# Band queries and keys projected once with a lane permutation on VectorE, PSUM banks given out singly, mask products on quarters of the array

## The chip, the cores and the metric

The program runs on one core of a Trainium2 chip. A core has five engines that run their own instruction queues in order and meet only at semaphores: TensorE (PE, matrix products into PSUM), VectorE (DVE), ScalarE (ACT), GpSimd (POOL, no access to PSUM) and SyncE (SP, transfers). PSUM has eight banks of 512 fp32 columns on 128 partitions; this kernel uses six of them for short-lived fills and two for the attention context. The metric is the device time of one execution in microseconds.

## The reference

The input x holds 16 sequences of 256 tokens with 128 features. Eight residual steps follow one another, each on the layer norm of x:

```
x = x + band_attention(norm(x))       # 16 heads of 64, bias, rotary (half-split), window of 128 keys back
x = x + ffn0(norm(x))                 # silu(gate) * up, hidden 384
x = x + causal_attention(norm(x))     # 16 heads of 8, rotary
x = x + ffn0(norm(x))
x = x + chunk_attention(norm(x))      # 16 heads of 8, rotary, chunks of 64 tokens
x = x + ffn1(norm(x))                 # hidden 352, operands quantised to FP4 in blocks of 16
x = x + lowrank_attention(norm(x))    # 16 heads, rank 32
x = x + ffn1(norm(x))
```

The rotary embedding of the band attention is `x * cos + concat(-x2, x1) * sin` over the 64 features of a head, where x1 and x2 are its lower and upper 32 features. Scores outside the window are -1e30 before the softmax.

## The kernel before

Work is cut into units: one unit is one kind of attention ("band", "causal", "chunk", "lowrank", and "end" for the last FFN) for one sequence, so 5 x 16 units. A unit has steps in stages: "forward" and "finish" (the FFN that lies ahead of its attention), "operands" (norm, queries, keys, values), "maxima" (a first pass of scores, whose negated row maxima are taken), "back" (scores again, transposed, with the mask and the maxima added in PSUM; exponentials; products with the values) and "tail" (denominators, scaling, output projection). The FFNs ahead of causal and chunk units are ffn0, those ahead of lowrank and end units are ffn1.

Nothing is ordered by hand. `make_plan` simulates the five engines once at build time with the durations of `work` and the waits of `needs`: at each step it takes, of the stages whose next step is ready, the one with the smallest start + PER_UNIT x unit - LEAD[engine][stage][kind]. What comes out is one fixed list of steps per engine (`ORDER`), and for every fill of PSUM its slot. A slot is a pair of banks (1024 columns), there are three (SLOTS), and a fill takes a whole slot even where it writes 256 columns. A fill on PE waits until the step in `released_by` of the slot's last user is done.

Band operands: for each of 8 chunks (two heads each) a step `qk` writes four products of 128 x 256 on PE: queries, queries with the halves of each head swapped (a second copy of the weights, rows permuted on the host), keys, keys swapped. Each product is three matmuls (high and low part of fp32), so 12 for a chunk. DVE (L1242) adds the bias and multiplies by the cosine or sine table in four instructions of 256 columns, POOL (L986) adds the two parts into `band_r`, ACT (L1007) casts them into `band_rb` for the first pass of scores. `band_r` has two buffers, `band_rb` one, so the cast of the next unit waits for this unit's last score fill. DVE runs two chunks ahead of POOL at most (`band_sum`).

Scores: a fill of the first pass ("score", six for a band unit) begins with two mask products (`mm_mask`, one for each bank, 128 x 128 by 512 or 256 columns), then comes a product for each head on 64 rows of the array, even heads on the upper and odd heads on the lower 64, each into a bank of its own. DVE takes the maxima (L1201). The last fill is followed on POOL by `parts` (L937 to L940, the maxima split in three bf16 parts), on PE by `nm` (a transpose). The fills of the second pass ("S", for each group g of four heads one wide and one narrow) have the same mask products, then keys x queries in fp32 and the maxima, and ACT takes the exponential (L1087). "V" is the product with the values and the row sums (`one_col`).

## Time and profile before

| | us |
|---|---|
| median of 3 runs (2148.47 to 2153.92) | 2152.45 |
| the profiled execution | 2152.07 |
| its span, first to last instruction | 2150.2 |
| PE busy | 1789.7 |
| DVE busy | 1345.8 |
| POOL busy | 978.6 |
| ACT busy | 808.8 |

The profile comes from one execution. "Busy" is the time in which an engine had an instruction in work; PEld is the weight load of PE, which overlaps its products. PEclk is the granted TensorE clock as a share of 2.4 GHz; the engine has two levels, 1.2 and 2.4 GHz, so 0.90 means a fifth of the time at 1.2. Products are pipelined, and the durations of single ones overlap: the time from start to start tells what one costs.

### The profile page before, as it was taken

The numbers are of one execution on the slowest core, as the hardware profiler recorded it, in microseconds if no ns is written. First come the engines' busy times: TensorE is split into PE (matmuls) and PEld (weight loads), VectorE is DVE, ScalarE is ACT, GpSimd is POOL, SyncE is SP. The second block draws the span as 40 slices with busy tenths as digits, with TensorE's granted clock in tenths as the row PEclk, the third lists the DMA queues.
The fourth block names the chain that finished last, engine by engine and source line by source line (L and its number), as shares of the span: only waits on it lengthen the run. The fifth ranks groups of instructions, "written<-read, shape, count | busy, mean of one in ns | idle before, by whom it ended". The sixth has DMA issues, their size and how long they took to land.

```text
span 2150.2 us, 51747 instructions
## 1 busy us (share of the span) xinstructions
PE 1789.7 (83%) x21261; PEld 1250.9 (58%) x21261; DVE 1345.8 (63%) x2753; ACT 808.8 (38%) x1303; POOL 978.6 (46%) x1362
## 2 busy tenths in 40 slices
PE   4899889999999998879999997777776778888883
PEld 4566565666666666655555555667665455555553
DVE  4555555555555543574555555677876788888873
ACT  2333333333333332324444444333333444444441
POOL 3333222333332222453333435689997455555543
PEclk9999999999999999989999999888998788888886
DMA  4000000000000000023333332233443223323310
GB/s 161 1 1 1 1 2 1 1 1 1 1 1 1 1 1 1 16 56 74 64 78 71 75 75 61 60 74 78 91 87 65 46 62 65 65 65 65 65 21 8
DMA packets 167465, 89.54 MB, mean 42 GB/s; under 512 B 9393, under 2 KB 165810, under 8 KB 166978
## 3 DMA queue, kind: packets, MB, share of 16 engines
q1 hardware_dynamic: 167010, 85.70, 18.4%
q8 instruction: 172, 2.82, 0.6%
q14 instruction: 59, 0.48, 0.1%
q0 software_dynamic: 224, 0.54, 0.1%
HBM read 46.36 MB, written 39.85 MB: 40 GB/s over the span
## 4 chain that ended last, share of the span: by engine, by line
PE 51%; DVE 27%; ACT 7%; POOL 7%; issue 6%; DVEq 0%; POOLq 0%; ACTq 0%
PE slots L1327 38%; DVE nmx L1201 12%; PE ctx_ps L1327 10%; DVE rope_part L1242 4%; ACT probs L1087 3%; DVE rope_part L1166 2%; PE slots L1615 2%; ACT ctxT L1007 1%; DVE ctxT L1303 1%; DVE rope_part L1167 1%; POOL xn L922 1%; PE slots L1394 1%; ACT band_va L1023 1%; POOL band_rb L645 1%; DVE band_r L1167 1%
## 5 line engine op out<-in xcount | busy, mean ns | idle before, releaser
L1087 ACT ACTIVATE probs<-slots 128x1024 f32<-128x1024 f32 (+1 forms) x416 | 356.1, 892 | 322.0 <-PE slots L1327 318.8
L1201 DVE TENSOR_REDUCE nmx<-slots 128x8 f32<-128x1024 f32 (+2 forms) x352 | 407.7, 1216 | 102.8 <-PE slots L1327 101.2
L1327 PE MATMUL slots<-band_r 64*64 64x64 bf16 (+4 forms) x5120 | 393.6, 263 | 80.5 <-DVE nmx L1201 41.7
L1327 PEld LDWEIGHTS slots<-band_r 64*128 64x128 bf16 (+2 forms) x5120 | 194.6, 120 | 254.3 <-issue 129.8
L1242 DVE SCALAR_TENSOR_TENSOR rope_part<-slots,bias_qk,rope_band 128x256 f32<-128x256 f32 x512 | 212.3, 477 | 197.3 <-PE slots L1327 176.4
L1327 PE MATMUL ctx_ps<-probs,band_va 64*32 64x64 f32 (+4 forms) x5120 | 260.5, 313 | 42.3 <-issue 19.4
L986 POOL TENSOR_TENSOR band_r<-rope_part 128x512 f32<-128x512 f32 x128 | 164.5, 1285 | 250.9 <-DVE rope_part L1242 250.9
L1327 PE MATMUL slots<-mask,ident_bf 128*128 128x256 bf16 (+1 forms) x896 | 217.2, 324 | 46.9 <-DVE nmx L1201 17.7
L1327 PE MATMUL slots<-nmT,pick 64*128 64x256 bf16 (+2 forms) x2560 | 218.7, 241 | 2.7 <-issue 2.7
L1327 PEld LDWEIGHTS ctx_ps<-probs,band_va 128*32 128x32 f32 (+2 forms) x5120 | 145.3, 118 | 125.6 <-issue 62.8
L900 POOL TENSOR_TENSOR var_eps<-mean_var,eps 128x2 f32<-128x2 f32 x128 | 29.2, 228 | 393.4 <-DVE mean_var L1129 393.4
L1327 PE MATMUL slots<-xT,band_qk 128*128 128x256 f32 x1536 | 200.0, 288 | 8.2 <-DVEq L1248 6.1
L1327 PEld LDWEIGHTS slots<-xT,band_qk 128*128 128x128 f32 x1536 | 188.0, 191 | 19.7 <-DVEq L1248 13.6
L1007 ACT ACTIVATE ctxT<-ctx_ps 128x512 f32<-128x512 f32 (+1 forms) x112 | 87.4, 781 | 169.2 <-PE ctx_ps L1327 169.2
L922 POOL TENSOR_SCALAR band_va<-x,mean_var,rstd 128x128 f32<-128x128 f32 x128 | 100.8, 794 | 86.0 <-PE slots L1368 65.9
L1007 ACT ACTIVATE band_rb<-band_r 128x512 bf16<-128x512 f32 x128 | 79.4, 630 | 157.0 <-POOL band_r L986 157.0
L1327 PEld LDWEIGHTS slots<-mask,ident_bf 128*128 128x128 bf16 x896 | 54.9, 97 | 133.8 <-issue 44.9
L1166 DVE SCALAR_TENSOR_TENSOR rope_part<-band_va,slots 128x352 f32<-128x352 f32 (+2 forms) x128 | 68.6, 536 | 81.9 <-ACT band_va L1023 55.5
L1327 PEld LDWEIGHTS slots<-nmT,pick 64*128 64x128 bf16 (+1 forms) x2560 | 102.9, 104 | 11.5 <-issue 2.9
L922 POOL TENSOR_SCALAR xn<-x,mean_var,rstd 128x128 f32<-128x128 f32 x128 | 103.6, 816 | 2.9 <-POOL rstd L901 2.8
L937 POOL CAST nm<-nmx 128x64 bf16<-128x64 f32 x64 | 15.1, 236 | 179.0 <-PE slots L1573 92.7
L901 POOL TENSOR_TENSOR rstd<-var_eps,minus_half 128x2 f32<-128x2 f32 x128 | 91.5, 715 | 10.0
(181 smaller groups left out, 2947.5 us busy)
## 6 DMA issues: line engine op xcount, KB each, us to landing
band_r<-scratch SPq DMA_DIRECT2D x192, 192.0 KB, 4.5
scratch<-parts SPq DMA_DIRECT2D x96, 192.0 KB, 2.2
scratch<-parts SPq DMA_DIRECT2D x96, 128.0 KB, 2.1
scratch<-parts SPq DMA_DIRECT2D x96, 64.0 KB, 1.8
x<-in_x SPq DMA_DIRECT2D x16, 128.0 KB, 4.5
out<-x SPq DMA_DIRECT2D x16, 128.0 KB, 1.8
band_r<-in_band_qk_a SPq DMA_DIRECT2D x1, 1024.0 KB, 6.4
band_va<-in_band_qk_b SPq DMA_DIRECT2D x1, 1024.0 KB, 10.3
```

Source lines behind the costliest of these rows:

```text
L900: link(nc.gpsimd.tensor_tensor(var_eps[:, b], mean_var[:, b, :, 1], eps[:], ALU.add))
L901: nc.gpsimd.tensor_tensor(rstd[:, b], var_eps[:, b], minus_half[:], ALU.pow).then_inc(rstd_ready, 1)
L922: nc.gpsimd.tensor_scalar(xn[:, t, :], x[:, b, t, :], mean_var[:, b, t, 0:1], rstd[:, b, t:t + 1], ALU.subtract, ALU.mult).then_inc(xn_rea ...
L986: nc.gpsimd.tensor_tensor(band_r[:, b % RING, j], part[:, 0], part[:, 1], ALU.add).then_inc(band_sum, 1)
L1007: return nc.scalar.activation(dst, src, ACT.Copy)
L1087: nc.scalar.activation(probs[:, g % 2, step[2], :, 0:width], slot(u, step).rearrange("p (a n) -> p a n", a=2)[:, :, 0:width], ACT.Exp, sca ...
L1166: link(nc.vector.scalar_tensor_tensor(g_out, t_in, 1.0, gate, ALU.add, ALU.mult))
L1167: nc.vector.tensor_tensor(h_out, g_out, up, ALU.mult).then_inc(free_sem(u, ("ffn", i)), 1)
L1201: nc.vector.tensor_reduce(dst, src, axis=AX.X, op=ALU.max, negate=True).then_inc(free_sem(u, step), 1)
L1242: nc.vector.scalar_tensor_tensor(rope_part[:, c % 2, rot, qk, :], slot(u, step)[:, o:o + TOK], bias_qk[:, j, 2 * qk + rot:2 * qk + rot + 1 ...
L1327: return nc.tensor.matmul(o, lhsT, rhs, start=start, stop=stop, skip_group_check=shared)
L1615: last = nc.tensor.transpose(B[:, g * P:(g + 1) * P], ctxT[:, g, t * P:(t + 1) * P], ident[:])
```

## The change

1. **Band queries and keys are projected once.** `qk` now writes two products of 128 x 256 (6 matmuls) into one bank. ACT adds the bias and writes `biased` (two activations of 256 columns, new), POOL multiplies by the cosine (step `cos`, new, 128 x 512), DVE swaps the halves with a lane permutation and multiplies by the sine (step `sin`: STREAM_SHUFFLE and TENSOR_TENSOR, both 128 x 512, instead of four SCALAR_TENSOR_TENSOR of 256), POOL adds as before (now part of `sin`). The permutation reaches 32 lanes, so the host permutes the features of a head, with which the halves lie 16 lanes apart; queries and keys have the same order, and scores don't change by it. `biased` has two buffers, `turned` has one.
2. **Weights**: the staged and split band weights are half as many (2 x 512 KB instead of 2 x 1024 KB).
3. **PSUM is given out in single banks.** A fill for which `narrow` is true takes one of six banks, any other takes a pair. A fill may wait for two earlier ones. There is a semaphore for each pair and each bank.
4. **Mask products on quarters.** Instead of one product of 128 x 128 for each bank there are two of 64 x 64; the four of a fill lie on the four quarters of the array.
5. **The plan's numbers**: the table LEAD, PER_UNIT and the durations for the changed steps are new, and with them the order on every engine.

```diff
-                steps.append(("qk", j))
+                steps += [("qk", j), ("cos", j), ("sin", j)]
...
-        "qk": [("pe", 1.43), ("dve", 1.56), ("pool", 1.21)] if big else [("pe", 0.72 if low else 1.43)],
+        "cos": [("pool", 1.21)],
+        "sin": [("dve", 1.3), ("pool", 1.21)],
+        "qk": [("pe", 0.72), ("act", 0.74)] if big else [("pe", 0.72 if low else 1.43)],
...
-        "operands": {"band": 4.447, "causal": 7.702, "chunk": 18.901, "lowrank": 57.299},
+        "operands": {"band": 0.0, "causal": 0.38, "chunk": -0.093, "lowrank": 3.926},
...
+def narrow(kind, step):
+    name = step[0]
+    if name == "v":
+        return kind != "band"
+    if name == "qk":
+        return kind in ("band", "lowrank")
+    if name == "ffn":
+        return step[1] == 2 and AHEAD[kind] == "ffn0"
+    return name in ("xT", "down", "nm", "den", "rden", "ctx", "ctxT", "out")
...
+                    if step[0] == "cos":
+                        j = step[1]
+                        c = b * CHUNKS + j
+                        if c >= 2:
+                            pool.wait_ge(band_sum, c - 1)
+                        pool.wait_ge(biased_ready, c + 1)
+                        released(pool, u, ("qk", j))
+                        nc.gpsimd.tensor_tensor(rope_part[:, c % 2, 0], biased[:, c % 2], rope["band"][:, 0:1, :].to_broadcast([P, 2, TOK]),
+                                                ALU.mult).then_inc(cosine_ready, 1)
...
+                    if kind == "band" and name == "qk":
+                        j = step[1]
+                        c = b * CHUNKS + j
+                        if c >= 2:
+                            act.wait_ge(band_sum, c - 1)
+                        act.wait_ge(front_full, FRONT_NO[u, step] + 1)
+                        for qk in range(2):
+                            nc.scalar.activation(biased[:, c % 2, qk], slot(u, step)[:, TOK * qk:TOK * (qk + 1)], ACT.Identity,
+                                                 bias=bias_qk[:, j, qk:qk + 1]).then_inc(free_sem(u, step) if qk else biased_ready, 1)
...
-                        for rot in range(2):
-                            for qk in range(2):
-                                o = 512 * qk + TOK * rot
-                                nc.vector.scalar_tensor_tensor(
-                                    rope_part[:, c % 2, rot, qk, :], slot(u, step)[:, o:o + TOK],
-                                    bias_qk[:, j, 2 * qk + rot:2 * qk + rot + 1], rope["band"][:, rot, :],
-                                    ALU.add, ALU.mult).then_inc(part_ready, 1)
...
+                        nc.vector.stream_shuffle(turned[:].rearrange("p q n -> p (q n)"),
+                                                 biased[:, c % 2].rearrange("p q n -> p (q n)"), HALVES_SWAPPED).then_inc(turn_ready, 1)
+                        dve.wait_ge(turn_ready, c + 1)
+                        nc.vector.tensor_tensor(rope_part[:, c % 2, 1], turned[:], twice(rope["band"][:, 1, :]), ALU.mult).then_inc(sine_ready, 1)
...
-                    o = bank.rearrange("p (h w) -> p h w", w=width)[:, :, columns]
-                    rhs = mask[:, allowed].unsqueeze(1).to_broadcast([P, heads, allowed.stop - allowed.start])
-                    mm(o, ident_bf[:], rhs, True, False, shared=True)
+                    for half in range(2):
+                        rows, at = (slice(HALF * i, HALF * i + HALF) for i in (half ^ par, half))
+                        o = bank[at].rearrange("p (h w) -> p h w", w=width)[:, :, columns]
+                        rhs = mask[rows, par, allowed].unsqueeze(1).to_broadcast([HALF, heads, allowed.stop - allowed.start])
+                        mm(o, ident_bf[rows, rows], rhs, True, False, shared=True)
```

How the order moves. First PE in the middle of the band stage; `xT,band_qk` is a unit's projection, `band_r` and `nmT` the second pass of scores, `band_rb` the first. Before, from the last narrow fill of the second pass on (96 matmuls are all eight chunks):

```order
L1327 MATMUL slots<-mask,ident_bf 128x256 x2
L1327 MATMUL slots<-band_r 128x128 x2
L1327 MATMUL slots<-nmT,pick 128x128 x2
L1327 MATMUL slots<-band_r 128x128 x2
L1327 MATMUL slots<-nmT,pick 128x128 x2
L1327 MATMUL slots<-xT,band_qk 128x256 x96
L1327 MATMUL ctx_ps<-probs,band_va 64x256 x2
```

After, from the next unit's transposed norm on (six matmuls are one chunk):

```order
L1426 MATMUL slots<-ident,xn 128x128 x2
L1385 MATMUL slots<-xT,band_qk 128x256 x6
L1630 MATMUL slots<-ident_bf,nm 128x128 x2
L1385 MATMUL slots<-xT,band_qk 128x256 x18
L1385 MATMUL slots<-mask,ident_bf 64x512 x4
L1385 MATMUL slots<-band_r 128x256 x2
L1385 MATMUL slots<-nmT,pick 128x256 x2
L1385 MATMUL slots<-band_r 128x256 x2
L1385 MATMUL slots<-nmT,pick 128x256 x2
L1385 MATMUL slots<-xT,band_qk 128x256 x18
```

The projection has moved from behind the second pass to its head, and lies between its fills.

POOL in the band stage, from the rstd of one unit on; `rope_part` is the chunk's rotary work. Before:

```order
L901 TENSOR_TENSOR rstd<-var_eps,minus_half 128x2
L986 TENSOR_TENSOR band_r<-rope_part 128x512 x8
L900 TENSOR_TENSOR var_eps<-mean_var,eps 128x2
L901 TENSOR_TENSOR rstd<-var_eps,minus_half 128x2
L922 TENSOR_SCALAR xn<-x,mean_var,rstd 128x128 x2
```

After, a piece of one unit:

```order
L1027 TENSOR_TENSOR rope_part<-biased,rope_band 128x512
L1037 TENSOR_TENSOR band_r<-rope_part 128x512
L1027 TENSOR_TENSOR rope_part<-biased,rope_band 128x512
L1037 TENSOR_TENSOR band_r<-rope_part 128x512
L941 TENSOR_TENSOR var_eps<-mean_var,eps 128x2
L942 TENSOR_TENSOR rstd<-var_eps,minus_half 128x2
```

Each chunk has two POOL instructions of 512 columns where it had one.

PE at the end of the band stage; `int_gu` and `int_d` are ffn0, ahead of the causal units. Before, in the last band unit's second pass:

```order
L1327 MATMUL slots<-int_d,rope_part 128x128 x6
L1327 MATMUL slots<-xTf,int_gu 128x256 x12
L1368 MATMUL slots<-ident,band_va 128x128 x2
L1327 MATMUL slots<-mask,ident_bf 128x256 x2
L1327 MATMUL slots<-band_r 128x128 x2
L1327 MATMUL slots<-nmT,pick 128x128 x2
```

After, behind that second pass:

```order
L1385 MATMUL slots<-int_d,rope_part 128x128 x6
L1385 MATMUL slots<-band_o,ctxT 128x128 x16
L1426 MATMUL slots<-ident,xn 128x128 x2
L1385 MATMUL slots<-xTf,int_gu 128x256 x12
L1385 MATMUL slots<-xT,causal_qkv 128x256 x12
L1385 MATMUL slots<-causal_qkv,xT 128x128 x6
```

Before, fifteen ffn0 stand between the maxima of the last band unit and those of the first causal unit; after, three and a half do, and the rest lie between the causal units. Counted in the order of PE by where the transpose `nm` of each unit stands (ffn0 and ffn1 in each stretch):

| stretch of PE's order | before | after |
|---|---|---|
| last band `nm` to first causal `nm` | 15 ffn0 | 3 ffn0 |
| first causal to first chunk | 9 ffn0 | 15 ffn0 |
| first chunk to first lowrank | 8 ffn0, 15 ffn1 | 13 ffn0, 5 ffn1 |
| first to last lowrank | 15 ffn1 | 25 ffn1 |
| after the last lowrank | 2 ffn1 | 2 ffn1 |

## Rows read from the trace of the kernel before

**Rows 1.** Windows: length, PE, PEld, DVE, ACT, POOL busy, clock, DMA share, GB/s

```profile
551.05:601.58 50.53, 47.33 (x440) 32.37 (x440) 26.15 (x58) 16.76 (x27) 15.35 (x20) 1.00 0.01 1
803.50:947.40 143.90, 117.78 (x1056) 90.47 (x1057) 75.33 (x190) 40.84 (x84) 57.48 (x84) 0.94 0.07 16
947.40:1299.60 352.20, 317.99 (x3778) 191.97 (x3778) 199.50 (x370) 160.44 (x261) 134.53 (x213) 1.00 0.34 72
1299.60:1675.00 375.40, 275.17 (x6435) 239.92 (x6434) 277.23 (x657) 136.58 (x253) 294.75 (x407) 0.88 0.36 74
1675.00:2086.90 411.90, 329.79 (x3295) 213.03 (x3292) 334.17 (x558) 197.30 (x290) 218.32 (x318) 0.86 0.28 58
2086.90:2150.20 63.30, 29.43 (x235) 22.60 (x233) 29.51 (x61) 15.71 (x25) 25.94 (x36) 0.69 0.02 7
```

**Rows 2.** POOL's cast of the maxima: all 64, then the third and last band unit's

```profile
L937 POOL CAST nm<-nmx x64: 230/236/238, 62.1 to 2086.9; 128x64 bf16<-128x64 f32 x64
...
131.96 0.24 POOL L937 CAST nm<-nmx 128x64 bf16<-128x64 f32 x1 [7.11 <-PE slots L1573]
...
803.55 0.24 POOL L937 CAST nm<-nmx 128x64 bf16<-128x64 f32 x1 [10.10 <-PE slots L1573]
```

**Rows 3.** Groups by line and shape: busy us, mean ns, idle before

```profile
L1242 DVE SCALAR_TENSOR_TENSOR rope_part<-slots,bias_qk,rope_band 128x256 f32<-128x256 f32 x512 | 212.3, 477 | 197.3 <-PE slots L1327 176.4 <-DVE rope_part L1242 20.9
L1327 PE MATMUL slots<-xT,band_qk 128*128 128x256 f32 x1536 | 200.0, 288 | 8.2 <-DVEq L1248 6.1 <-DVE xT L1142 2.0
L986 POOL TENSOR_TENSOR band_r<-rope_part 128x512 f32<-128x512 f32 x128 | 164.5, 1285 | 250.9 <-DVE rope_part L1242 250.9
L1201 DVE TENSOR_REDUCE nmx<-slots 128x4 f32<-128x1024 f32 x256 | 296.7, 1215 | 22.3 <-PE slots L1327 20.9 <-DVE rope_part L1258 0.2 <-DVE band_va L643 0.2
L1007 ACT ACTIVATE xT<-slots 128x256 fp32r<-128x256 f32 x64 | 24.6, 384 | 39.3 <-PE slots L1368 38.8
L1303 DVE TENSOR_TENSOR ctxT<-slots,ctxT 128x512 f32<-128x512 f32 x64 | 40.0, 682 | 36.0 <-PE slots L1327 36.0
L1327 PE MATMUL slots<-xTf,int_gu 128*128 128x256 f32 x384 | 59.9, 305 | 2.9 <-DVE nmx L1201 1.8 <-DVE xTf L1142 0.2
L1327 PE MATMUL slots<-int_d,rope_part 128*128 128x128 f32 x384 | 53.8, 294 | 4.5 <-DVE rope_part L1167 3.8 <-DVE x L1317 0.3 <-DVE ctxT L1303 0.2
```

**Rows 4.** Timeline of PE in a band unit's second pass: start us, us

```profile
614.63 0.86 PE L1327 MATMUL ctx_ps<-probs,one_col 128*32 128x256 f32 x16
615.42 0.60 PE L1327 MATMUL slots<-mask,ident_bf 128*128 128x512 bf16 x2
615.96 0.70 PE L1327 MATMUL slots<-band_r 64*128 64x256 f32 x4
...
617.25 0.39 PE L1327 MATMUL slots<-mask,ident_bf 128*128 128x256 bf16 x2
617.57 0.49 PE L1327 MATMUL slots<-band_r 64*128 64x128 f32 x4
```

**Rows 5.** Timeline of DVE in a band unit's projection: two chunks

```profile
627.24 1.66 DVE L1242 SCALAR_TENSOR_TENSOR rope_part<-slots,bias_qk,rope_band 128x256 f32<-128x256 f32 x4 [0.21 <-DVE rope_part L1242]
...
629.11 1.66 DVE L1242 SCALAR_TENSOR_TENSOR rope_part<-slots,bias_qk,rope_band 128x256 f32<-128x256 f32 x4 [0.21 <-DVE rope_part L1242]
```

**Rows 6.** By line, ns min/median/max; then DVE and POOL at one moment

```profile
L939 POOL CAST nm<-nmx_d x64: 236/236/956, 62.7 to 2087.5; 128x64 bf16<-128x64 f32 x64
L639 DVE TENSOR_TENSOR band_va<-band_va x32: 424/679/949, 1370.5 to 2114.3; 128x256 f32<-128x256 f32 x32
...
1452.05 0.89 DVE L639 TENSOR_TENSOR band_rb<-band_r,band_rb 128x704 f32<-128x704 f32 x1
1452.08 0.95 POOL L939 CAST nm<-nmx_d 128x64 bf16<-128x64 f32 x1
```

**Rows 7.** Lowrank stretch by tile, DVE fourth number: band_rb, then band_va

```profile
1675.00:2086.90 411.90, 6.02 (x28) 2.91 (x28) 52.03 (x90) 0.00 (x0) 89.05 (x104) 0.86 0.28 58
...
1675.00:2086.90 411.90, 72.30 (x960) 27.96 (x960) 69.33 (x112) 18.26 (x42) 51.17 (x70) 0.86 0.28 58
```

180 lines of the change are left out of this document (105 added, 75 removed).

## The prediction

> **What bounds the kernel now.** I read the busy time by window first, with windows cut at POOL's casts of the row maxima (L937), of which each attention unit has one. The first comes at 62.1 us, the third at 131.96, the sixteenth, of the last band unit, at 803.55, the last at 2086.9 [rows 2]. In the middle of the band stage a unit takes 50.53 us, and PE is busy 47.33 of them at full clock, DVE 26.15, ACT 16.76, POOL 15.35 [rows 1]: PE is the bound there, at 0.937 of the time. The causal stretch is the same (318.0 of 352.2 us, 0.903, clock 1.00). The chunk stretch isn't: POOL has 294.8 and DVE 277.2 of 375.4 us; nor is the lowrank stretch, where DVE has 334.2 and PE 329.8 of 411.9 us, at a granted clock of 0.86 [rows 1]. So PE work that goes counts in the first 1300 us; behind that the order counts.
>
> **Projection.** Half of 1536 matmuls go. Each costs 200.0/1536 = 0.130 us of PE [rows 3], 48 go for a unit: 6.25 us. On DVE a chunk had four instructions in 1.66 us, and came every 1.87 us [rows 5]. Now a chunk has two ACT activations of 256 columns at 0.384 (an activation of that size from PSUM, [rows 3]), so 0.77 us, 6.1 for a unit; ACT then has 23 of some 44 us, and its cost is covered. On POOL a second instruction of 1.285 us joins the first [rows 3]: 10.3 us more for a unit, POOL then 25.6 us. On DVE the product with the sine has 512 columns, 0.68 us by the nearest row, L1303 [rows 3]. The trace has no STREAM_SHUFFLE. Its lower bound is half of that row, 0.34, its upper bound POOL's 1.285 for as many columns; it reads one operand of the same width on DVE, so I take 0.65, nearest to the DVE row. That is 1.33 us for a chunk; at the bounds DVE would have 1.02 or 1.97, and for a unit 24 to 31 us, still not the bound.
>
> **The new chain.** POOL's two instructions and DVE's product are on one chain, and I don't think that they overlap. At 1452.05 a DVE product with two SBUF operands starts; POOL's cast of 0.24 us that starts 0.03 behind it takes 0.95, until the other has ended; and the same DVE product of 256 columns takes between 0.424 and 0.949 us [rows 6]. Before, the rotary products of DVE had one operand in PSUM and POOL's sums kept to 1.285. Now each chunk has a DVE product with two SBUF operands, and POOL reads SBUF all the time. So a chunk takes 2 x 1.285 + 0.68 = 3.25 us, not 2.57, and eight take 26.0 us, not 20.6.
>
> The Trainium skill, page SBUF — State Buffer, section Who interferes with whom, states just this: a DVE instruction with two SBUF inputs and a GpSimd instruction that reads SBUF exclude one another for the whole instruction. The trace agrees, with the 0.95 us above. A rule that lets them run beside each other gives the first rival's time below.
>
> What stands in that chain: the first chunk's matmuls and activations (0.78 + 0.77, so 1.5 us), eight chunks (26.0), and, as `band_rb` is single and PE's order has most of a unit's projection behind the last unit's scores, the rest of DVE's work, 26.15 - 8 x 1.66 = 12.9 us (six maxima at 1.215 and the scaling). Sum 40.4; the maxima's split on POOL, the casts and the exponentials that stand behind casts in ACT's queue add some 3.5. I take a band period of 44 us. PE alone gives less: 47.33 - 6.25 - 2.7 (masks, below) = 38.4, over 0.937 is 41.0 us. So in the band stage the bound moves from PE to the POOL/DVE chain, and PE idles an eighth of the time.
>
> **Masks.** The two products of a wide fill take 0.54 us to the start of what follows (615.42 to 615.96), of a narrow one 0.32 (617.25 to 617.57) [rows 4]. Quarters on different rows and columns can run at once if they behave as the row sums do, 16 records of `one_col` on four column strips in 0.79 us [rows 4]. Then a wide fill needs one pass: half of 0.54, and something for two more loads: 0.32, saved 0.22. Narrow: saved 0.12. Bounds: nothing saved (two pairs one behind the other), or 0.1 us more for each fill for the extra loads, and at best half, 0.27. A band unit has 10 wide and 4 narrow fills: 2.7 us; a causal unit 2 and 12: 1.9 us.
>
> A rule against it: the Trainium skill, page TensorEngine Tiling (Array Packing), section Key Properties, says that a change of tiling mode drains the array. The rows have such a change already, from 128 x 128 masks to products on 64 rows, inside the 0.54 us, so I count no further one.
>
> **Setup.** The split of the band weights is halved. It was in the first 62 us; DVE and ACT work on 2 x 1024 columns less. I take 4 us off, bounds 0 and 8.
>
> **Order and banks.** The table of stretches in the change shows where FFNs go. One ffn0 costs PE (59.9 + 53.8)/32 = 3.55 us [rows 3], with its transposes 4. One ffn1 costs DVE some 10: 52.0 + 69.3 us on two tiles for 15 of them is 8.1 [rows 7], the rest I estimate. Its PE cost lies between an ffn0's 4 and these 10; I take 6.5. Single banks (`narrow`) take away waits for slots; of these PE has few before (idle 8.2 us before the projection, [rows 3]), so I give them nothing beyond the shares below.
>
> **The sum**, stretch by stretch:
> - to the last band cast: 62.1 - 4 + 70 (the first two periods fill the pipeline and stay: 131.96 - 62.1) + 13 x 44 = 700 (before 803.5)
> - last band to first causal cast: PE had 117.8 us with 15 ffn0. Without 12 of them (48), a tail that now lies earlier (5) and masks (2.7) 62 are left; at 0.9 that is 70 (143.9)
> - causal: (318.0 - 9 x 4)/16 - 1.9 = 15.7 a unit; 16 x 15.7 + 15 x 4 = 311; over 0.903: 345 (352.2)
> - chunk: PE 275.2 - 10 x 6.5 + 5 x 4 = 230, above DVE's and POOL's, which lose ten ffn1; at 0.88: 262 (375.4)
> - lowrank: DVE 334.2 + 10 x 10 = 434. At the share of before, 0.81, it takes 535; DVE and PE are loaded more evenly, so 0.83: 523 (411.9)
> - end: 63 (63.3)
>
> Together 1963 us of span. The profiled execution took 2152.07, 1.9 more than its span and within 0.4 of the median of the runs, 2152.45; so I forecast **1965 us**, 187 less than before.
>
> **Rivals.**
> 1. *The products don't exclude each other.* A chunk then takes 2.57 us and PE bounds the band: 13 x (44 - 41) = 39 us less; with a lowrank stretch as tight as the causal one (434/0.88 = 493) 30 less again: 1896. For it: the order interleaves chunks and fills, so a late chunk may hide. Against it: rows 6. 0.20.
> 2. *The quarters give nothing.* This is the case where a part doesn't do what it says. Causal + 1.9 x 16/0.9 = 34 us; the band unit's PE goes to 41.1, over 0.937 is 43.9, so little there, 1 us a unit: 2012. 0.12.
> 3. *The plan was made with wrong prices.* It counts 1.3 and 1.21 us for steps that block each other, and ACT, strictly in order, has activations of the projection between exponentials. Band period 48 (+52), lowrank at 0.81 and a lower clock (+20): 2037. 0.15.
> 4. *Slower.* The projection chain doesn't overlap with the second pass at all: in some units of the new order ACT does all eight chunks of a unit in a row. If all units went so, a period would be 26.0 + 12.9 + some 20 for the second pass, about 59; and where PE idles that long its clock falls (0.86 and 0.94 in stretches where PE is busy 0.80 and 0.82 of the time, [rows 1]), which adds 3. At 62 the span is 234 more, so 2199. It is slower from a band period of about 59 on. Against it: PE's order has chunks between the fills in most units. 0.08.
>
> The forecast itself has 0.45, with 1930 to 2010 as its own range.
>
> **Range and chances.** 1890 to 2075 holds the forecast, rivals 1 and 2 and nearly all of 3. A measurement tells 0.3%, 6.5 us, from no change. Faster 0.88, within 0.3% 0.03, slower 0.09 (rival 4, and the tail of 3).
>
> **What would show it.** The last band cast near 700 us, band periods of 44, PE busy some 38.5 in one; POOL's or DVE's instruction in pairs of which one lasts longer than alone (DVE's product above 0.68, POOL's above 1.285) shows the exclusion, both at their lengths refutes it. Mask groups: from their start to what follows 0.32 instead of 0.54. Causal periods near 21.5 us, chunk 16, lowrank near 35. The forecast is wrong if the first pass waits long for the last cast in every unit, or if the lowrank stretch passes 550 us.

## The result, and the profile after

The changed kernel takes 2207.52 us (median of 4 runs, 2198.63 to 2212.92) against 2152.42 of the kernel before beside it: ratio 1.0249, 95% interval 1.0221 to 1.0278. It is slower by 2.5%, where 1965 us had been forecast. The profiled execution took 2198.63 us, the shortest of the four, with a span of 2196.8.

By stretch, cut at the same casts of the row maxima (before, forecast, after):

| stretch | before | forecast | after |
|---|---|---|---|
| start to last band cast | 803.5 | 700 | 844.0 |
| to the first causal cast | 143.9 | 70 | 65.8 |
| to the first chunk cast | 352.2 | 345 | 359.7 |
| to the first lowrank cast | 375.4 | 262 | 304.3 |
| to the last lowrank cast | 411.9 | 523 | 541.9 |
| to the end | 63.3 | 63 | 81.1 |

The bands are 144 us over the forecast, all that follows 90 us over it, and 6 us over before.

Windows of the changed kernel (columns as in [rows 1]): three neighbouring band units, then the stretches of the table.

```profile
477.80:535.50 57.70, 50.03 (x515) 35.43 (x510) 35.89 (x66) 25.00 (x49) 29.21 (x30) 0.97 0.01 1
535.50:606.10 70.60, 51.97 (x483) 34.35 (x481) 47.04 (x77) 33.89 (x64) 52.90 (x48) 0.86 0.00 1
606.10:628.70 22.60, 22.31 (x274) 13.36 (x272) 6.11 (x6) 9.25 (x15) 1.07 (x5) 0.98 0.01 1
...
844.00:909.80 65.80, 51.17 (x490) 38.00 (x490) 31.03 (x63) 17.04 (x33) 27.40 (x36) 0.88 0.17 42
909.80:1269.50 359.70, 325.75 (x4401) 211.69 (x4402) 217.34 (x421) 170.42 (x280) 142.09 (x227) 0.97 0.31 69
1269.50:1573.80 304.30, 220.59 (x5936) 192.48 (x5938) 195.05 (x453) 110.55 (x203) 192.47 (x289) 0.88 0.40 88
1573.80:2115.70 541.90, 393.74 (x3688) 257.30 (x3688) 398.84 (x787) 215.16 (x337) 321.91 (x450) 0.82 0.21 46
2115.70:2196.80 81.10, 47.19 (x406) 33.50 (x404) 32.79 (x80) 26.36 (x39) 34.42 (x45) 0.77 0.03 9
```

Band casts no longer come evenly: gaps of 57.7, 70.6 and 22.6 us, 50.3 on average, as long as the 50.53 of [rows 1]. PE is busy (50.03 + 51.97 + 22.31)/3 = 41.4 us of such a unit, 5.9 less than before. It waits 8.9 instead of 3.2. So the matmuls went, and waiting took their place; the granted clock, 1.00 before, is 0.86 in the long gap. The full period of 13 units, from the third cast to the last, is (844.0 - 159.7)/13 = 52.6 us.

Groups by line and shape (busy us, mean ns, idle before), the new operations of a chunk:

```profile
L1027 POOL TENSOR_TENSOR rope_part<-biased,rope_band 128x512 f32<-128x512 f32 x128 | 201.2, 1572 | 105.9 <-ACT biased L1100 105.9
L1305 DVE TENSOR_TENSOR rope_part<-turned,rope_band 128x512 f32<-128x512 f32 x128 | 174.7, 1365 | 4.4
L1037 POOL TENSOR_TENSOR band_r<-rope_part 128x512 f32<-128x512 f32 x128 | 162.8, 1272 | 43.9 <-DVE rope_part L1305 19.2 <-issue 10.8 <-ACT biased L1100 4.1
L1100 ACT ACTIVATE biased<-slots,bias_qk 128x256 f32<-128x256 f32 x256 | 106.8, 470 | 151.9 <-POOL band_r L1037 91.6 <-PE slots L1385 59.6
L1302 DVE STREAM_SHUFFLE turned<-biased 128x512 f32<-128x512 f32 x128 | 94.4, 738 | 0.6
```

The timeline of DVE in one of the bursts (start us, us):

```profile
546.44 1.77 DVE L1305 TENSOR_TENSOR rope_part<-turned,rope_band 128x512 f32<-128x512 f32 x1
548.67 0.01 DVE L1302 LOAD_MASK_SELECT turned<-biased  x1 [0.46 <-ACT biased L1100]
548.69 0.75 DVE L1302 STREAM_SHUFFLE turned<-biased 128x512 f32<-128x512 f32 x1
549.47 1.76 DVE L1305 TENSOR_TENSOR rope_part<-turned,rope_band 128x512 f32<-128x512 f32 x1
```

and that of POOL there:

```profile
547.61 1.73 POOL L1027 TENSOR_TENSOR rope_part<-biased,rope_band 128x512 f32<-128x512 f32 x1
549.42 1.26 POOL L1037 TENSOR_TENSOR band_r<-rope_part 128x512 f32<-128x512 f32 x1
550.64 1.72 POOL L1027 TENSOR_TENSOR rope_part<-biased,rope_band 128x512 f32<-128x512 f32 x1
```

A chunk comes every 3.03 us (547.61 to 550.64), against 1.87 in [rows 5]. DVE's product at 549.47 starts 0.05 us behind POOL's sum, which keeps to 1.26 us; the product takes 1.76 and lies across the start of POOL's next product, which takes 1.72. So it is the one that starts later which lasts longer, each time: DVE's product beside the sum, then POOL's product beside DVE's. The sums (L1037) stay between 1.26 and 1.31 us in the whole kernel.

PE around that burst, and the quarter masks in the next pass:

```profile
538.08 1.66 PE L1385 MATMUL slots<-xT,band_qk 128*128 128x256 f32 x12
542.63 0.64 PE L1385 MATMUL slots<-mask,ident_bf 64*64 64x512 bf16 x4 [2.90 <-ACT biased L1100]
543.21 1.23 PE L1385 MATMUL slots<-band_r 64*128 64x256 f32 x4
...
603.52 0.64 PE L1385 MATMUL slots<-mask,ident_bf 64*64 64x512 bf16 x4 [8.92 <-ACT band_rb L1058]
...
611.77 0.41 PE L1385 MATMUL slots<-mask,ident_bf 64*64 64x512 bf16 x4
612.11 0.70 PE L1385 MATMUL slots<-band_r 64*128 64x256 f32 x4
...
613.39 0.30 PE L1385 MATMUL slots<-mask,ident_bf 64*64 64x256 bf16 x4
613.63 0.49 PE L1385 MATMUL slots<-band_r 64*128 64x128 f32 x4
```

The same four products take 1.23 us behind the wait of 2.90, where the granted clock is 0.50 (the lower of its levels, 1.2 GHz), and 0.70 at 612.11, where it is 1.00. The longest wait is that of 8.92 us at 603.52: the first pass of scores waits for the last cast of a chunk. It comes once in three units (also at 452.17 with 7.59 us and at 756.30 with 8.92), in the long gap. There PE's order has all eight projections of a unit, from 572.89 on, behind one second pass and ahead of the next, so that their chain runs to 603.4 with no second pass beside it. A wide mask group now takes 0.34 us to what follows, a narrow one 0.24, against 0.54 and 0.32 in [rows 4].

### The profile page after: what moved, and what is told of

Same layout as the page of the kernel before. It is cut to its first block, busy times and chain, and to the rows that moved or that the text cites. A ratio compares the mean times of both kernels' runs of the same rounds, so it can differ in the third digit from the quotient of the medians.

```text
span 2196.8 us, 52690 instructions
## 1 busy us (share of the span) xinstructions
PE 1708.4 (78%) x21389; PEld 1186.9 (54%) x21389; DVE 1383.7 (63%) x2625; ACT 900.9 (41%) x1559; POOL 1171.4 (53%) x1490
## 4 chain that ended last, share of the span: by engine, by line
PE 45%; DVE 27%; POOL 9%; issue 8%; ACT 6%; DMA 1%; SPq 1%; DVEq 0%; POOLq 0%; ACTq 0%
PE slots L1385 32%; PE ctx_ps L1385 10%; DVE nmx L1261 10%; POOL band_r L1037 3%; ACT probs L1147 2%; POOL rope_part L1027 2%; DVE rope_part L1305 2%; PE slots L1452 2%; DVE rope_part L1226 1%; DVE turned L1302 1%; DVE stats L1186 1%; PE slots L1426 1%; ACT band_r L1058 1%; DVE band_rb L679 1%; DVE band_rb L676 1%
## 5 line engine op out<-in xcount | busy, mean ns | idle before, releaser
L1385 PE MATMUL slots<-band_r 64*64 64x64 bf16 (+4 forms) x5120 | 412.5, 273 | 104.8 <-DVE nmx L1261 67.0
L1027 POOL TENSOR_TENSOR rope_part<-biased,rope_band 128x512 f32<-128x512 f32 x128 | 201.2, 1572 | 105.9 <-ACT biased L1100 105.9
L1385 PE MATMUL slots<-mask,ident_bf 64*64 64x256 bf16 (+1 forms) x1792 | 166.4, 361 | 91.1 <-ACT band_rb L1058 41.9
L1385 PE MATMUL slots<-nmT,pick 64*128 64x256 bf16 (+2 forms) x2560 | 213.4, 240 | 0.0
L1037 POOL TENSOR_TENSOR band_r<-rope_part 128x512 f32<-128x512 f32 x128 | 162.8, 1272 | 43.9 <-DVE rope_part L1305 19.2
L1305 DVE TENSOR_TENSOR rope_part<-turned,rope_band 128x512 f32<-128x512 f32 x128 | 174.7, 1365 | 4.4
L1100 ACT ACTIVATE biased<-slots,bias_qk 128x256 f32<-128x256 f32 x256 | 106.8, 470 | 151.9 <-POOL band_r L1037 91.6
L1385 PEld LDWEIGHTS slots<-mask,ident_bf 64*64 64x64 bf16 x1792 | 52.3, 105 | 186.8 <-issue 114.9
L1058 ACT ACTIVATE ctxT<-ctx_ps 128x512 f32<-128x512 f32 (+1 forms) x112 | 87.5, 781 | 107.3 <-PE ctx_ps L1385 107.2
L963 POOL TENSOR_SCALAR band_va<-x,mean_var,rstd 128x128 f32<-128x128 f32 x128 | 107.6, 848 | 37.6 <-PE slots L1426 35.5
L1385 PE MATMUL slots<-xT,band_qk 128*128 128x256 f32 x768 | 118.7, 307 | 8.5 <-DVE xT L1202 5.0
L1385 PEld LDWEIGHTS slots<-xT,band_qk 128*128 128x128 f32 x768 | 104.5, 206 | 20.4 <-issue 9.8
```

Of the source, the lines that this page charges most:

```text
L963: nc.gpsimd.tensor_scalar(xn[:, t, :], x[:, b, t, :], mean_var[:, b, t, 0:1], rstd[:, b, t:t + 1], ALU.subtract, ALU.mult).then_inc(xn_rea ...
L1027: nc.gpsimd.tensor_tensor(rope_part[:, c % 2, 0], biased[:, c % 2], rope["band"][:, 0:1, :].to_broadcast([P, 2, TOK]), ALU.mult).then_inc( ...
L1037: nc.gpsimd.tensor_tensor(band_r[:, b % RING, j], part[:, 0], part[:, 1], ALU.add).then_inc(band_sum, 1)
L1058: return nc.scalar.activation(dst, src, ACT.Copy)
L1100: nc.scalar.activation(biased[:, c % 2, qk], slot(u, step)[:, TOK * qk:TOK * (qk + 1)], ACT.Identity, bias=bias_qk[:, j, qk:qk + 1]).then_ ...
L1305: nc.vector.tensor_tensor(rope_part[:, c % 2, 1], turned[:], twice(rope["band"][:, 1, :]), ALU.mult).then_inc(sine_ready, 1)
```

## The experiments

The median of the kernel before moved between 2152 and 2158 us from one set of runs to the next, so the table gives each kernel's ratio to the runs of before beside it. The fourth and fifth columns are of the profiled execution: the last band cast, and the span left behind it.

| kernel | ratio | 95% interval | last band cast | rest |
|---|---|---|---|---|
| before | 1 | | 803.5 | 1346.7 |
| after | 1.0249 | 1.0221 to 1.0278 | 844.0 | 1352.8 |
| b_quarters | 0.9937 | 0.9913 to 0.9962 | 796.0 | 1341.6 |
| b_quarters_banks | 1.0383 | 1.0346 to 1.0420 | 793.7 | 1442.4 |
| a_old_lead | 1.0965 | 1.0920 to 1.1009 | 923.8 | 1433.0 |
| a_no_sine | 1.0092 | 1.0060 to 1.0123 | 804.8 | 1365.0 |
| a_sum_only | 0.9868 | 0.9847 to 0.9890 | 754.7 | 1368.1 |
| a_full_mask | 1.0416 | 1.0377 to 1.0454 | 858.3 | 1381.3 |
| a_interleaved | 1.0538 | 1.0492 to 1.0585 | 838.2 | 1428.8 |
| a_interleaved_filled | 1.0574 | 1.0551 to 1.0596 | 844.3 | 1434.8 |
| a_products_swapped | 1.0459 | 1.0427 to 1.0492 | 870.9 | 1382.9 |
| a_repriced | 1.0276 | 1.0232 to 1.0320 | 863.9 | 1354.0 |
| a_late_old_lead | 1.0435 | 1.0407 to 1.0464 | 841.2 | 1408.7 |
| a_paired_banks | 1.1055 | 1.1030 to 1.1080 | 854.8 | 1526.2 |
| b_qb_same_order | 0.9850 | 0.9825 to 0.9876 | 789.9 | 1333.2 |
| a_same_order | 1.0468 | 1.0445 to 1.0491 | 923.9 | 1332.6 |
| own_band_old_late | 1.0083 | 1.0054 to 1.0111 | 844.0 | 1333.8 |
| own_products | 0.9651 | 0.9623 to 0.9679 | 772.7 | 1311.2 |
| order_old_late | 0.9794 | 0.9771 to 0.9816 | 793.1 | 1320.1 |
| order_old_late_2 | 0.9491 | 0.9467 to 0.9515 | 740.8 | 1307.7 |

### Parts of the change on the kernel before

**b_quarters** takes the masks alone.

```
-                    o = bank.rearrange(...)[:, :, columns]
-                    mm(o, ident_bf[:], rhs, True, False, shared=True)
+                    for half in range(2):
+                        rows, at = (slice(HALF * i, HALF * i + HALF) for i in (half ^ par, half))
+                        mm(bank[at]..., ident_bf[rows, rows], rhs, True, False, shared=True)
```

> The kernel before with one part of the change alone: the mask products on quarters of the array. Order, banks and projections are those of before. Theory A (part is worth what its fills show): in the changed kernel a wide mask fill lasted 0.34 us from its start to the next product's, against 0.54 before, a narrow one 0.23 against 0.32; a band unit has 10 wide and 4 narrow fills, so 2.0 + 0.4 = 2.4 us a unit, 38 us in 16 units, and about half as much a unit in the causal stretch, 15 us: about 2100 us. Rival: the freed time of TensorE falls where it waits for VectorE anyway: 2140 to 2152 us, with the band period still 50.5.

It gave 0.6%, some 13 us. The 2143.6 us lie in the rival's range, but its unchanged period of 50.5 isn't found, and theory A's 2100 isn't reached. The windows of two band units:

```profile
595.40:644.80 49.40, 45.35 (x469) 32.35 (x470) 26.13 (x58) 16.67 (x26) 15.35 (x19) 1.00 0.01 1
644.80:694.20 49.40, 45.33 (x469) 32.35 (x470) 26.14 (x58) 16.67 (x26) 15.35 (x19) 1.00 0.01 1
```

The timeline of PE has the wide fills of the second pass 4.91 us apart; in the kernel before they came 5.20 apart, from 615.42 in [rows 4] to the first line here:

```profile
620.62 0.61 PE L1327 MATMUL slots<-mask,ident_bf 128*128 128x512 bf16 x2
```

```profile
611.94 0.41 PE L1327 MATMUL slots<-mask,ident_bf 64*64 64x512 bf16 x4
...
616.85 0.41 PE L1327 MATMUL slots<-mask,ident_bf 64*64 64x512 bf16 x4
```

The period falls from 50.5 to 49.4: that is the four second-pass pairs, 4 x 0.29 = 1.2. The six wide fills of the first pass give nothing, though PE does them faster, since each is followed by a maximum of 1.215 us on DVE [rows 3]. The causal stretch gives nothing either: PE is busy 309.9 us of it instead of 318.0, and it lasts 352.0 instead of 352.2.

**b_quarters_banks** adds the single banks and the rule by which the plan gives them out (`narrow`, with its semaphores); the band's projection keeps a pair.

> The kernel before with the quarter mask products and with the banks given out singly; band queries and keys still with four projections, LEAD and prices of the plan as before. The plan orders the work anew, since narrow fills take one bank. Theory A (banks alone bring nothing, and only the order that the planner makes of them can move the time): within 1.5% of the kernel with quarters alone, so 2070 to 2130 us. Theory B (the old LEAD was fitted to the old rule for the slots, and a new order under it is worse): over 30 us slower than with quarters alone. Theory C (single banks free TensorE of waits for a slot): over 20 us faster than quarters alone.

**b_qb_same_order** has the same operations and banks, but each engine's steps in the order of the kernel before, held fixed: a step is a candidate only if it is the next in a stored list.

```
+                if (u, step) != FIXED[eng][len(order[eng])][1:]:
+                    continue
```

> The kernel before with quarter masks and single banks, and the order of every engine's steps held fixed as in the kernel before; only which bank a fill takes follows the new rule. Under the same LEAD but with a free order it took 2240, with quarters alone 2144. Theory A (the 96 us were the order that the plan made of the new rule, not the banks): 2125 to 2150, and chunk, lowrank and end together near 850 again. Theory B (the banks themselves cost, for instance since a wide fill needs two neighbours free at once): over 2180.

Theory B of the first stood: 1.038. Theory A of the second: 0.985, another 0.9% below the quarters alone. The banks don't cost, they give a little (causal stretch, first to last cast: 331.4 to 325.0). The 5.4% between the two kernels are the plan's order alone, made from the same numbers under another rule for the slots. **a_paired_banks**, the reverse (`narrow` always false in the changed kernel, with its own LEAD), says it again:

> The changed kernel with every fill taking two banks, as the kernel before did; LEAD, operations and prices as in the changed kernel, the order made anew by the plan. Theory A (single banks let TensorE run ahead, and with pairs it waits for slots): last band cast 20 us or more later than 844, TensorE's waits for ScalarE's biased chunk longer. Theory B (single banks bring the band nothing; with three pairs it has the same order of chunks): last band cast within 15 us of 844. The later stretches come to another order, so the whole (2200 to 2310) says less than the band stretch.

The last band cast agrees with theory B, 854.8 and 844.0; the whole is 8% above the changed kernel, and 173 of its 184 us of span lie behind the bands. The order of the bands isn't that of the changed kernel, though: the casts come evenly here, 51.2 us apart in the middle, without a wait of PE over 2.2 us there, and the period is no shorter. So it isn't the unevenness that costs.

### The changed operations in old orders

**a_old_lead** is the changed kernel with the old LEAD and PER_UNIT.

```
-        "operands": {"band": 0.0, "causal": 0.38, "chunk": -0.093, "lowrank": 3.926},
+        "operands": {"band": 4.447, "causal": 7.702, "chunk": 18.901, "lowrank": 57.299},
 (and so all of LEAD)
-PER_UNIT = 0.0185
+PER_UNIT = 0.01
```

> The changed kernel, with the numbers LEAD and PER_UNIT of the kernel before: all changed operations, another order. Theory A (the new order is what costs): the band casts come evenly again, without pairs of units 70 and 23 us apart, the band period falls to 44 to 46 us and the time to 2060 to 2130. Theory B (the operations cost the time, the order is only their consequence): the chunk pace stays 3.0 us, the band period 50 or more, the time 2200 or more. Both keep VectorE's sine product at about 1.4 us and GpSimd's cosine product at 1.6 us on average.

**a_same_order** holds the old order fixed instead; ScalarE's new step is put where its matmuls end.

> All changed operations in the order of the kernel before, held fixed; the new ScalarE step of a chunk is put where its products of TensorE end in that order. With the old LEAD and a free order it took 2364, with a band period of 58.0. Theory A (the chain of chunks costs 8 us a unit where it lies behind the second pass, as one block; the rest of the time is the order's): band period 57 to 58, last band cast about 920, behind it 1340 to 1360 as in the kernel before, the whole 2260 to 2285. Theory B (ScalarE's and GpSimd's new work disturbs the later stages too): the stretches behind the last band cast over 1400 us together.

Theory B of the first, A of the second: band period 58.0, last band cast 923.8 and 923.9. In the fixed order the rest is 1332.6, the same as without the projection's change (1333.2); so the projection touches nothing behind the bands. This pair, b_qb_same_order and a_same_order, prices the new projection by itself in the old order: 0.9850 to 1.0468, a loss of 135 us between the medians, all of it ahead of the last band cast (789.9 to 923.9). The window of one unit of a_old_lead:

```profile
576.00:634.00 58.00, 44.67 (x420) 28.53 (x421) 31.07 (x51) 22.64 (x42) 27.93 (x27) 0.82 0.00 1
```

and PE's timeline in it, from the block of eight projections on:

```profile
596.69 5.95 PE L1385 MATMUL slots<-xT,band_qk 128*128 128x256 f32 x48
...
612.08 0.28 PE L1630 MATMUL slots<-ident_bf,nm 128*128 128x128 bf16 x2 [1.50 <-ACT biased L1100]
615.04 2.92 PE L1385 MATMUL slots<-band_v,xT 128*128 128x512 f32 x6 [2.68 <-DVE rden L1354]
...
623.21 0.40 PE L1385 MATMUL slots<-rdT,wide_pick 64*128 64x256 bf16 x2 [3.16 <-DVE ctxT L1361]
625.17 0.64 PE L1385 MATMUL slots<-mask,ident_bf 64*64 64x512 bf16 x4 [1.56 <-ACT band_rb L1058]
```

All eight chunks are projected by 602.6, but the first pass, which needs the last cast, starts at 625.2. The chain runs on in between, and the last unit's scaling stands behind its chunks in DVE's queue and ACT's. Before, the same block cost PE 12 us and the chain 8 x 1.87 = 15; now it costs PE 6 and the chain 24. What PE saved it waits for, and more, at half clock.

### What the chain costs in the changed kernel's own order

**a_no_sine** leaves out the sine product, **a_sum_only** the cosine product too.

```
-   stream_shuffle(turned, ...)
-   tensor_tensor(rope_part[:, c % 2, 1], turned[:], twice(rope["band"][:, 1, :]), ALU.mult)
+   stream_shuffle(rope_part[:, c % 2, 1], ...)
```

> The changed kernel in its own order, with the sine product of the bands left out: the shuffle writes its result where the product would have been written. Only VectorE's operation that reads two SBUF tiles beside GpSimd's products is gone. Theory A (VectorE's and GpSimd's products hold each other up): GpSimd's cosine product falls from 1.72 to 1.26 us although nothing of GpSimd's was changed, the pace of the chunks from 3.03 to about 2.55, the stretch to the last band cast by about 60 us (8 x 0.5 us a unit), the time to 2130 to 2150. Theory B (GpSimd's 1.72 us is its own length for an operand that is broadcast): the cosine product stays at 1.72, the pace near 3.0, the time within 15 us of 2207. Theory C (the order makes the stalls, not the products): the pace falls as in A, but the time falls by less than 20 us.

> The changed kernel in its own order, with both products of the bands left out: ScalarE adds the bias, VectorE shuffles, GpSimd adds the two. GpSimd's work on a chunk falls from 3.0 to 1.3 us, VectorE's from 2.5 to 0.75; TensorE's and ScalarE's stay. Prices the whole chain of the chunks, where leaving out the sine product alone gave 30 us. Theory A (the chain of chunks is what TensorE waits for in the band stretch): last band cast at 720 to 750 instead of 844, band period 43 to 45 as forecast, the whole 2090 to 2120. Theory B (TensorE waits mostly for the first pass, VectorE's maxima and the tail, which are untouched): last band cast 780 to 805, little better than the 804.8 without the sine product, the whole 2150 to 2175. Both: the stretches behind the bands change by less than 20 us.

```profile
L1027 POOL TENSOR_TENSOR rope_part<-biased,rope_band 128x512 f32<-128x512 f32 x128 | 163.4, 1276 | 116.9 <-ACT biased L1100 116.9
```

Without DVE's product POOL's, which nothing else was done to, takes 1276 ns on average instead of 1572 (a_no_sine, group by line), although the shuffle still runs beside it. That settles the exclusion. Leaving the sine product out, which takes away its own time too, is worth 39 us of band stretch, 844.0 to 804.8, less than the 60 of theory A; the whole came to 2178, above the 2130 to 2150 of that theory. Both products are worth 89 us, 844.0 to 754.7, and 3.7% of the whole: nearer to theory A, though the last band cast (720 to 750 expected) and the whole of 2126 (2090 to 2120) both lie above its ranges.

**a_full_mask** takes the quarters out of the changed kernel, its order unchanged.

> The changed kernel in its very order, with the mask products over the full array as before. On the kernel before the quarters gave 13 us, of which 1.1 us a band unit (four wide and four narrow second-pass fills, 4 x 0.29), while the six first-pass fills gave nothing since VectorE's maxima set their pace. Theory A (the same here): 2215 to 2225. Theory B (in the changed kernel TensorE waits more, so the quarters give less): within 5 us of 2207. Theory C (busier TensorE holds its clock): faster than 2205.

1.0416 against 1.0249, so they are worth 36 us here, three times what they gave before. No theory had that. The profiled executions put 14 us of it in the bands, 13 in the causal stretch (372.8 against 359.7, where PE is busy 341.6 us instead of 325.8) and 17 in the chunk stretch (321.4 against 304.3). The 17 aren't all the masks': a_no_sine, which behind the bands has the operations and the order of the changed kernel, took 314.3 there, at a clock of 0.83 instead of 0.88.

### Other orders

**a_repriced** asks whether the plan's wrong prices did it (a chunk counted 1.3 us on DVE, where it takes 2.1 to 2.5).

> The changed kernel, with the prices of the band's steps in its plan set to what the trace showed (cosine 1.76, shuffle and sine product 2.53, sum 1.29, ScalarE's bias pair 0.90, projection 0.81, score 0.67, second pass 1.62 and 0.96), and LEAD found anew for these prices. Every instruction is unchanged, only the order differs. Theory A (the order was fitted to prices 1.2 us too low a chunk, and that is what costs): 2130 to 2175. Theory B (no order of this kind gains back what the longer chunk costs): within 1% of 2207.

Theory B: 1.0276, no better than the changed kernel. The plan's own arithmetic had promised 32 us (its simulated end with the new prices is 2039.7 us under the changed kernel's LEAD and 2007.5 under the new one).

**a_late_old_lead** puts the old LEAD under the chunk, lowrank and end steps only.

> The changed kernel with the old LEAD for the kinds chunk, lowrank and end, and its own for band and causal. Tells what the new order does behind the bands. Theory A (the new order moves feed-forward work from the chunk into the lowrank stretch, where TensorE's clock is lower and VectorE fuller, and loses by it): chunk, lowrank and end together, 954 us in the changed kernel and 911 with all numbers old, come to 900 to 925, the whole to 2155 to 2180. Theory B (the sum of the work is the same and only its place changes): within 15 us of 2207.

Neither: the chunk stretch grew from 304.3 to 380.8 us and the end from 81.1 to 107.2, the lowrank stretch shrank from 541.9 to 504.9, and the rest grew to 1408.7. **own_band_old_late** did the same with the order itself, not the numbers that make it.

> The changed kernel's operations and its own order of all band steps, word for word; behind the bands the steps follow one another on each engine as in the kernel before. Theory A (each stretch stands alone): last band cast 840 to 850 as in the changed kernel, the rest 1325 to 1345 as in b_qb_same_order (1333), the whole 2170 to 2195. Theory B (the changed kernel's order behind the bands is as good as the old one, only laid out otherwise): within 10 us of 2207.

Theory A, by all its numbers: 844.0, 1333.8 and a median of 2173.4 us. So LEAD's numbers aren't a description of an order. In these runs they held for one set of prices and rules, and every kernel that took them over to another was slower than the one they came from.

**a_interleaved** lets TensorE project chunk j only behind fill j of the unit before's second pass.

```
+        if kind == "band" and name == "qk" and u:
+            yield u - 1, ("S", step[1] // 2, step[1] % 2), "pe"
```

> The changed kernel with one rule more in its plan, and the band's operand steps given 3 us more lead: TensorE may project chunk j of a band unit only after fill j of the unit before's second pass. So the eight projections are neither one block behind the second pass (as with the old numbers, period 58.0) nor a burst ahead of it (as in the changed kernel, gaps of 70, 23 and 58), but one to each fill. All operations and their lengths stay. Theory A (the chain of chunks, 8 x 3.03 = 24.3 us, costs only where TensorE has no other work beside it): the second pass, about 27 us of TensorE's time, covers it, and the band period falls from 50.4 on average to 46 to 49 us, the last band cast from 844 to 780 to 800. Theory B (the products' exclusion costs the same wherever they lie, since VectorE and GpSimd are needed by the pass too): period 50 to 52. The order of the later stages changes too, so the band stretch is what tells them apart; the whole by A is 2140 to 2190.

**a_interleaved_filled** repeats products of the scaling in it.

```
-                        for cc in range(2):
+                        for cc in (0, 1, 0, 1, 0, 1):
```

> The interleaved kernel, where TensorE does each of the four bands' scale products (the spread of the reciprocals) three times instead of once, with the same result: 16 more 64x256 products a unit, just where TensorE waits for VectorE ahead of the output projection. In the interleaved kernel that projection took 6.50 us behind four waits of 0.2 to 0.95 us, in the kernel before 3.84. Theory A (the granted clock falls to half after these waits, and that costs 2.7 us a unit): the projection takes 3.84 to 4.5 us, the band period falls from 50.2 to 47.5 to 49, the last band cast from 838 to 800 to 825, although work was added. Theory B (the repeated products lie on the path of the scale chain, VectorE waits for each, and the clock falls anyway at the fills before): period 50.5 to 52.

By their numbers both are theory B: period 50.2, last band cast 838.2, and 51.2 and 844.3 with the filling products. A window of a_interleaved, one unit:

```profile
592.00:642.60 50.60, 43.43 (x422) 30.19 (x423) 31.04 (x51) 22.21 (x42) 27.97 (x27) 0.90 0.00 1
```

PE's timeline at its output projection, with that of the kernel before ahead of it:

```profile
608.39 3.84 PE L1327 MATMUL slots<-band_o,ctxT 128*128 128x128 f32 x32
```

```profile
592.65 6.50 PE L1387 MATMUL slots<-band_o,ctxT 128*128 128x128 f32 x32 [0.95 <-DVE ctxT L1363]
```

and the same in a_interleaved_filled:

```profile
590.91 1.42 PE L1387 MATMUL slots<-rdT,wide_pick 64*128 64x256 bf16 x12 [0.46 <-DVE ctxT L1363]
593.21 6.10 PE L1387 MATMUL slots<-band_o,ctxT 128*128 128x128 f32 x32 [0.88 <-DVE ctxT L1363]
```

The second pass was dense now, from 599.74 on 27.5 us without a wait of PE, and the chain lay beside it. But the unit's end was left thin: the reciprocals, the scaling and the output projection with nothing between them, and the projection ran mostly at half clock (0.56 granted on average in these 6.5 us), 6.50 us where it takes 3.84 at full. Ahead of it PE waited five times in some 4 us, for 0.31 to 0.95 us. More products there didn't bring the clock back (6.10, at 0.61), but they didn't fill all: waits of 0.56, 0.46 and 0.88 us were left. So that remedy fell, and what the half clock costs a unit isn't shown by it. order_old_late and what follows it put other work there instead.

**a_products_swapped** removes the exclusion and leaves nothing out: DVE makes the cosine product, from PSUM as the kernel before did, POOL the sine product.

```
-   POOL: rope_part[:, c % 2, 0] = biased * cos
-   DVE:  turned = shuffle(biased); rope_part[:, c % 2, 1] = turned * sin
+   DVE:  rope_part[:, c % 2, 1] = shuffle(biased); rope_part[:, c % 2, 0, qk] = (slot + bias) * cos
+   POOL: rope_part[:, c % 2, 1] *= sin
```

> The changed kernel with the two products exchanged: VectorE makes the cosine product with the bias, straight from PSUM, in two instructions as the kernel before did (477 ns each), and the shuffle, while GpSimd makes the sine product in place and the sum. No VectorE instruction of the chunk then reads two SBUF tiles. The bank is freed by VectorE instead of ScalarE, so the plan differs at a few places. Theory A (exclusion gone): GpSimd's product takes 1.28 us, VectorE's two 0.48 each, the chunk pace is 2.55 us instead of 3.03, the last band cast 30 to 45 us earlier than 844 and the whole 2150 to 2180, as with the sine product left out. Theory B (what is gained on the pair is lost since the bank is held longer, until VectorE has read it): pace 2.55, but TensorE waits more for a bank, and the whole is over 2195.

The whole went up, by theory B's number, but not for its reason as far as I can tell: with another engine freeing the bank the plan made another order (band gaps of 78, 83 and 23 us), and two things had changed at once.

**order_old_late** and **order_old_late_2** combine what had held: products exchanged, chunk j behind fill j - 1, the steps behind the bands in the old order, held fixed.

> Products exchanged (as in a_products_swapped), projections interleaved with the second pass (chunk j one fill later than in a_interleaved), prices of the bands' steps by the trace, and behind the bands the order of the kernel before held fixed. Theory A (the loss behind the bands was the order's, and pace 2.55 with interleaving lets the chain lie beside the second pass): last band cast 740 to 790, behind it 1335 to 1365, the whole 2080 to 2150. Theory B (the band period stays at 50, since TensorE's clock falls in the thin stretch ahead of the output projection, as in a_interleaved): last band cast 830 or later, the whole 2170 to 2200.

> As order_old_late, with LEAD for the bands found by a search on the plan's own arithmetic: TensorE's output projection of a unit lies one fill earlier, and the last band units meet the causal ones earlier. Theory A: 20 to 40 us below order_old_late. Theory B (the plan's arithmetic doesn't know the clock, so what it gains isn't there on the chip): within 15 us of order_old_late.

**own_products** has the order of the second, but the change's own operations.

> The order of every engine as in order_old_late_2, held fixed, with the very operations of the changed kernel (GpSimd the cosine product, VectorE the sine product with two SBUF operands, the bank freed by ScalarE). Theory A (where the chain lies beside the second pass, its pace hardly counts): pace 3.03 us instead of 2.65, band period 44 to 45.5 instead of 43.6 to 45.1, the whole 2055 to 2080. Theory B (the exclusion costs its full price in any order: 8 x 0.4 = 3.2 us a unit): period 47 to 48, the whole 2095 to 2115.

order_old_late came to 2114.9 us, ratio 0.9794, in theory A's range, with its last band cast (793.1) just above the range and the rest (1320.1) below it. order_old_late_2 came to 2050.5, ratio 0.9491, 64 us lower, more than theory A's 20 to 40. own_products came to 2083.8, ratio 0.9651. order_old_late_2 is 5.1% faster than the kernel before and 7.4% faster than the changed one. Two band units of it, by window:

```profile
522.00:609.20 87.20, 81.01 (x834) 54.41 (x833) 47.91 (x108) 43.50 (x80) 50.19 (x53) 0.96 0.01 2
```

POOL's two operations of a chunk, in its timeline:

```profile
544.68 1.27 POOL L1213 TENSOR_TENSOR rope_part<-rope_part,rope_band 128x512 f32<-128x512 f32 x1
546.09 1.29 POOL L1217 TENSOR_TENSOR band_r<-rope_part 128x512 f32<-128x512 f32 x1
547.33 1.27 POOL L1213 TENSOR_TENSOR rope_part<-rope_part,rope_band 128x512 f32<-128x512 f32 x1
```

and PE's timeline at a unit's end:

```profile
566.86 0.60 PE L1566 MATMUL slots<-mask,ident_bf 64*64 64x512 bf16 x4
...
571.49 0.97 PE L1566 MATMUL slots<-xT,band_qk 128*128 128x256 f32 x6
572.78 3.81 PE L1566 MATMUL slots<-band_o,ctxT 128*128 128x128 f32 x32 [0.31 <-DVE ctxT L1542]
```

A unit takes 43.6 us here, PE is busy 40.5 of them, and in a row the chunks come every 2.65. The next unit's first fill (566.86) and one more chunk of projection (571.49) now stand ahead of the output projection, which begins there at 572.78 and runs at full clock, 3.81 us. It is the fill that has the half clock here (0.60 for its masks). With the change's own products, whose pace is 3.03, the last eight periods are 46.6 us on average against 44.1: 2.5 of the 3.0 us that the exclusion adds to eight chunks show, even in an order that mostly hides the chain. That lies between its two theories, by the period and by the whole.

So the 7.4% between the changed kernel and the best one split in three steps: 1.0249 to 1.0083 for the order behind the bands, to 0.9651 for the order of the bands, to 0.9491 for the exchange of the products. The middle step also moves where the last bands meet the causal units (22.6 of its us lie behind the last band cast), and the last one also changes which engine frees the bank, so it isn't the exclusion alone.

## Why the prediction was wrong

**The operations: right.** The pace of a chunk was put at 3.25 us, with the exclusion, and is 3.03. The shuffle was put at 0.65, and takes 0.74. DVE's sine product takes 0.69 when it is alone and up to 1.8 beside POOL, POOL's cosine product 1.26 alone and 1.72 beside DVE. A pair of activations takes 0.84 us, not 0.77. The mask groups came to 0.34 and 0.24, where 0.32 and 0.20 were forecast. Rival 1 (no exclusion) is refuted, and rival 2 (the quarters give nothing) too. One side sum was wrong and changed nothing: at its bounds DVE would have had 12.9 + 8 x 1.02 = 21 to 12.9 + 8 x 1.97 = 29 us a unit, not 24 to 31.

That agrees with the rule of the Trainium skill, page SBUF — State Buffer, section Who interferes with whom, which was cited ahead of the result; the timelines at 546.44 to 549.34 show it on both sides, as longer instructions and not as idle time. The drain at a change of tiling mode (the Trainium skill, page TensorEngine Tiling (Array Packing), section Key Properties) doesn't show as a cost: the group of four quarter products is shorter than that of the two full ones, 0.34 against 0.54. Both groups are followed by products of another mode, so no run here shows the drain by itself.

**The band period: the step that failed.** "What stands in that chain" added 1.5 + 26.0 + 12.9 + 3.5 to 44 us, as if the chain and DVE's other work were one row, and PE's second pass, some 20 us, always lay beside it. That holds only if the order puts it there. The changed kernel's doesn't: in every third unit all eight chunks lie behind one second pass and ahead of the next, PE waits 8.92 us for the last cast at 603.52, the granted clock is 0.82 from 580 to 606, and three units take 151 us. In the old order, where the chain lies so in every unit, the period is 58.0. Leaving both products out of the chain gave 89 us of the stretch back (a_sum_only), and another order of the bands alone, with the operations as they are, 71 (own_band_old_late to own_products, 844.0 to 772.7). Periods of 43.6 to 45 do exist, in order_old_late_2, with the operations of a chunk sped up, and 46.6 with them as they are, late in the stretch (47.8 over all 13 periods). So the forecast's number was near what the operations allow and had nothing in it for the order that they got, although the order stood in the document and rival 4 had read it: "ACT does all eight chunks of a unit in a row". Rival 4 was judged by how many units go so in full and given 0.08. Its time, 2199, is right by accident: it had the bands at a period of 62 and the rest at the forecast, where the trace has 50.3 and 90 us more behind them.

**Two smaller terms of the band stretch.** The first two periods were kept at 70 us and the first cast put at 58; they took 92 and 67.75, so the third cast came at 159.7, 32 us late. And 13 periods were all counted as steady ones, though in the kernel before the mean of the 13 is (803.55 - 131.96)/13 = 51.7 against 50.5: the units that also prepare the weights of the feed-forward take 54 to 57. That is 15 us that the forecast dropped. Together the stretch came 144 us late: 32 at the third cast and 13 x (52.6 - 44) = 112 behind it.

**Masks.** Each fill saves what was forecast, and a unit was given 2.7 us for it. On the kernel before it gave 1.1, as the first pass waits for DVE's maxima; that those six fills have cover was in the rows ([rows 3], 1215 ns each) and not in the sum. A causal unit was given 1.9 us, 30 in the stretch; b_quarters shows 8 us less of PE there and 0.2 less of time, and a_full_mask against the changed kernel 16 and 13.

**Setup.** 4 us were taken off, and the first cast came 5.6 us later than before. Its order had changed too, so the setup's own gain isn't told by that.

**Behind the bands.** Band to causal was right (70 forecast, 65.8). Causal was 15 us too low: its share was right, 325.75/359.7 = 0.906, but PE had 311 us in the sum and 325.75 in the trace, which is what the mask term took off too much. Chunk failed most: 262 forecast, 304.3 measured. PE's 220.6 us there are near the 230 of the sum, but they are 0.72 of the stretch and not 0.88. The 0.88 has no row as a busy share: PE had 275.17/375.4 = 0.73 before, DVE 0.74 and POOL 0.79, and 0.88 stands in [rows 1] only as the granted clock of that stretch. With 0.73 the sum would have given 314 us. So PE's share of before did hold there, and the step that failed is the share that was put in its place, some 50 us of the sum. Lowrank was 19 us too low, by two errors against each other: DVE has 398.8 us and not 434 (the ten ffn1 more cost it 6.5 us each, not 10), and its share is 0.74 and not 0.83, where it was 0.81 before. The end came 18 us over its 63, with 47.2 us of PE in it instead of 29.4. In the lowrank stretch the clock is 0.82. Two lines of the kernel before, then three of the changed one:

```profile
1896.20 0.39 PE L1327 MATMUL slots<-band_r 64*128 64x256 bf16 x4 [0.74 <-DVE nmx L1201]
1897.34 0.39 PE L1327 MATMUL slots<-band_r 64*128 64x256 bf16 x4 [0.74 <-DVE nmx L1201]
```

```profile
1829.95 1.03 PE L1385 MATMUL slots<-band_r 64*128 64x256 bf16 x8 [3.57 <-DVE nmx L1261]
1832.19 0.61 PE L1385 MATMUL slots<-band_r 64*128 64x256 bf16 x4 [1.21 <-DVE nmx L1261]
1833.33 0.61 PE L1385 MATMUL slots<-band_r 64*128 64x256 bf16 x4 [0.52 <-DVE nmx L1261]
```

Score fills stand there in a row, each behind a maximum of DVE, and take 0.61 us at half clock for what took 0.39. That costs nothing at this place: the fills start 1.14 us apart in both kernels, since DVE's maxima set their pace. What does cost in this stretch isn't shown. What the new order behind the bands costs in all is measured: with the old one there the ratio falls from 1.0249 to 1.0083, 34 us between the medians, and the rest in the profiled executions from 1352.8 to 1333.8. The other 70 us between 1334 and the forecast's 1263 no kernel here found; the lowest rest is 1307.7.

**Rival 3**, wrong prices in the plan, was the nearest in spirit (0.15, 2037). Prices by the trace and new numbers to go with them changed nothing, 1.0276. What the plan's arithmetic lacks isn't told by its prices alone; the half clock behind waits is one thing that it has no term for.

**What stays open.** Why the quarters save time in the changed kernel's causal stretch and not in that of the kernel before, why DVE's share fell in the lowrank stretch, why the added products didn't restore the clock in a_interleaved_filled, and how much of the 90 us of the band order is clock and how much waiting.

## What to carry to other kernels

An operation that leaves the bound engine is worth what the order lets it be: ask which chain its replacement makes, how long that chain is for one unit, and which work of the bound engine is placed beside it, and read this from the new order row by row before taking the sum of busy times. When a planner makes the order, hold the old order fixed first and change only operations; here this told in two kernels what eight with free orders could not, and a set of tuning numbers was worth nothing under a changed rule. The same operations in two orders were 13.6% apart (a_old_lead and own_products, 1.0965 and 0.9651), five times the effect that was to be measured. The planner's own simulated end (`MODEL_END` of each kernel) shows part of this ahead of any run: 1961.7 us for the kernel before, 2012.3 for b_quarters_banks, 2029.7 for a_paired_banks and 2031.5 for a_old_lead. It doesn't replace a run: for the changed kernel, whose prices lacked the exclusion, it is 1925.1.

## What the runs showed of the hardware

- DVE's product with two SBUF operands and POOL's instructions take turns: DVE's product takes 0.69 us alone and up to 1.8 behind a POOL sum that has started, POOL's product 1.26 alone and 1.72 behind DVE's; a DVE product with one operand in PSUM keeps 0.47 us and leaves POOL's at 1.28.
- A STREAM_SHUFFLE of 128x512 f32 takes 0.74 us, and POOL's instructions beside it keep their length (1.28 us in a_no_sine and order_old_late_2).
- Four products of 64x512 on the four quarters of the array take 0.34 us to the next product, two of 128x512 on the full array 0.54.
- PE's output projection of a band unit takes 3.84 us at full clock and 6.1 to 6.5 behind a few waits of 0.3 to 0.95 us, also when the waits are partly filled with short products.
